# Two-layer graph network on one core: basis values and window numbers of the first edge loop kept in PSUM

## The reference

```
p     = clip(edge_attr_2, 0, 1)                       # 400000 x 2
b     = max(1 - |p[:, :, None] - (0, .5, 1)| * 2, 0)  # hat functions, 400000 x 2 x 3
basis = einsum('ea,eb->eab', b[:, 0], b[:, 1])        # reshaped to 400000 x 9
messages = einsum('ek,ei,kio->eo', basis, x[src], weight)
out   = zeros.at[dst].add(messages) / max(degree, 1) + x @ root_w.T + root_b
x     = layernorm(x + out)
```

## Time and profile before

| | us |
|---|---|
| median of 3 runs | 12081.59 |
| lowest and highest run | 12078.36, 12100.39 |
| profiled execution: span | 11991.0 |
| of it, first edge loop, first gather to the end of the last one | 4691.3 |
| of it, second edge loop (window 5060 to 11960) | 6900 |
| PE busy | 7745.6 (65%) |
| DVE busy | 7532.1 (63%) |
| POOL busy | 6643.3 (55%) |
| ACT busy | 817.6 (7%) |

### The profile page before, as it was taken

How to read it: one execution, slowest core, us unless ns; L and a number is a source line. 1 busy time by engine, 2 the same in 40 slices (tenths; PEclk the granted TensorE clock), 3 DMA queues, 4 the chain that set the end, 5 groups by cost and what they waited for, 6 DMA issues and landing times. The chain is left out here.

```text
span 11991.0 us, 122458 instructions
## 1 busy us (share of the span) xinstructions
PE 7745.6 (65%) x35701; PEld 5552.3 (46%) x35701; DVE 7532.1 (63%) x14033; ACT 817.6 (7%) x1907; POOL 6643.3 (55%) x6757
## 2 busy tenths in 40 slices
PE   5777777777777777455555555555555555555555
PEld 5777777777777777322222222222222222222223
DVE  4333333333333333588888888888888888888887
ACT  0000000000000000000000000000000000000000
POOL 5777777777777777044444444444444444444443
PEclk5555555555555555577777777777777777777776
DMA  1000000000000000011111111111111111111111
GB/s 36 11 11 11 11 11 11 11 11 11 11 11 11 11 11 11 37 39 36 39 36 39 36 39 36 39 36 39 37 39 37 39 37 38 37 38 37 38 37 29
DMA packets 251980, 327.74 MB, mean 27 GB/s; under 512 B 110894, under 2 KB 160959, under 8 KB 251087
## 3 DMA queue, kind: packets, MB, share of 16 engines
q0 software_dynamic: 200000, 205.20, 9.1%
q1 hardware_dynamic: 51962, 122.31, 3.2%
HBM read 320.67 MB, written 6.40 MB: 27 GB/s over the span
## 5 line engine op out<-in xcount | busy, mean ns | idle before, releaser
L411 PE MATMUL sums_ps<-hot,spread 128*96 128x64 f32 (+1 forms) x18750 | 3183.6, 370 | 1075.5 <-DVE spread L361 1075.5
L411 PEld LDWEIGHTS sums_ps<-hot,spread 128*96 128x96 f32 (+1 forms) x18750 | 3068.2, 281 | 1221.4 <-DVE spread L361 650.7
L361 DVE TENSOR_TENSOR spread<-basis,rows 128x1440 f32<-128x1440 f32 x625 | 1039.8, 1664 | 3215.1 <-DMA rows<-in_x,idx_a 1902.4
L754 PE MATMUL radial_x<-edge_t,hidden 128*128 128x384 f32 x3750 | 1916.7, 664 | 1211.3 <-DVE edge_t L856 1121.4
L282 POOL DMA_INDIRECT rows<-table_dram,idx_a x1875 | 1772.3, 945 | 1484.6 <-DVE prods_y L856 889.6
L282 POOL DMA_INDIRECT rows<-in_x,idx_a x1875 | 2140.3, 1141 | 634.2 <-issue 533.3
L754 PE MATMUL radial_y<-edge_t,hidden 128*128 128x384 f32 x2500 | 1377.7, 689 | 1509.5 <-DVE prods_y L856 1509.5
L754 PEld LDWEIGHTS radial_x<-edge_t,hidden 128*128 128x128 f32 x3750 | 886.1, 252 | 1856.0 <-issue 920.2
L282 POOL DMA_INDIRECT rows<-in_x,idx_b x1250 | 1422.4, 1138 | 443.7 <-issue 342.8
L282 POOL DMA_INDIRECT rows<-table_dram,idx_b x1250 | 1188.9, 951 | 766.7 <-DVE prods_y L856 363.0
L754 PEld LDWEIGHTS radial_y<-edge_t,hidden 128*128 128x128 f32 x2500 | 555.7, 246 | 2273.4 <-DVE prods_y L856 2014.4
(11 more groups left out here) (121 smaller groups left out, 3794.7 us busy)
## 6 DMA issues: line engine op xcount, KB each, us to landing
dist<-in_edge_weight SPq DMA_DIRECT2D x625, 160.0 KB, 3.2
rows<-in_x,idx_a POOLq DMA_INDIRECT x1875, 2.4
rows<-table_dram,idx_a POOLq DMA_INDIRECT x1875, 2.5
rows<-in_x,idx_b POOLq DMA_INDIRECT x1250, 2.4
rows<-table_dram,idx_b POOLq DMA_INDIRECT x1250, 2.5
acc<-in_edge_attr SPq DMA_DIRECT2D x1, 4687.5 KB
table_dram<-edge_t SPq DMA_DIRECT2D x1, 4687.5 KB
acc<-in_edge_attr SPq DMA_DIRECT2D x1, 3125.0 KB
```

Of the source, the lines that this page charges most:

```text
L361: dve.tensor_tensor(spread[s][:, :, 0:K].rearrange("e t (k c) -> e t k c", c=C), basis[s][:, :, :].unsqueeze(3).to_broadcast([P, G, 9, C]) ...
L411: last = pe.matmul(sums_ps[s][0:m, c * WINDOW:(c + 1) * WINDOW], spread[s][:, j, c * CH:c * CH + m], hot[s][:, j, :], start=(j == 0 and c ...
L754: last = pe.matmul(radial[h][:, j, 0:R], hidden[s][:, (j0 + j) * P:(j0 + j + 1) * P], w2p[:, :], start=True, stop=True)
```

## The change

A seventh PSUM bank, `own_ps`, is added for the first edge loop. Its first 64 columns hold the row of window numbers, copied there once per pass (there is one pass); the next 3 x 45 columns hold the three buffers of `basis`. So `basis` is written to PSUM, `hot` reads `window` from PSUM and `rel_t` from SBUF, and `spread` reads `basis` from PSUM and `rows` from SBUF. `basis` itself still reads two views of `edge_t` in SBUF. The order of the instructions in the loop, the waits and the buffer counts stay as they are; ahead of the loop there is one copy of 64 elements and a wait for it.

```diff
         rows = ring("rows", [P, G, C])
-        basis = ring("basis", [P, G, 9])
         spread = ring("spread", [P, G, K + 1])
...
-        gathers_begun = sem("l0_gathers_begun")
+
+        own_ps = ctx.enter_context(nc.psum_tensor("own_ps", [P, 512], F32))
+        window_ps = own_ps[:, 0:WINDOW]
+        basis = [own_ps[:, WINDOW + n * 9 * G:WINDOW + (n + 1) * 9 * G].rearrange("e (t k) -> e t k", k=9) for n in range(SLOTS)]
+        gathers_begun, window_ready = sem("l0_gathers_begun"), sem("l0_window_ready")
...
-                dve.tensor_tensor(basis[s][:, :, :].rearrange("e t (a b) -> e t a b", b=3),
+                dve.tensor_tensor(basis[s].rearrange("e t (a b) -> e t a b", b=3),
                                   f[:, :, 0:3].unsqueeze(3).to_broadcast([P, G, 3, 3]),
                                   f[:, :, 3:6].unsqueeze(2).to_broadcast([P, G, 3, 3]), ALU.mult).then_inc(basis_ready, 1)
-                dve.tensor_tensor(hot[s][:, :, :], keep["window"][:, :].unsqueeze(1).to_broadcast([P, G, WINDOW]),
+                dve.tensor_tensor(hot[s][:, :, :], window_ps.unsqueeze(1).to_broadcast([P, G, WINDOW]),
                                   rel_t[:, tiles].unsqueeze(2).to_broadcast([P, G, WINDOW]), ALU.is_equal).then_inc(hot_ready, 1)
                 dve.wait_ge(basis_ready, done(g, u))
                 dve.wait_ge(rows_landed[s], filled(g, u, 16 * G))
                 dve.tensor_tensor(spread[s][:, :, 0:K].rearrange("e t (k c) -> e t k c", c=C),
-                                  basis[s][:, :, :].unsqueeze(3).to_broadcast([P, G, 9, C]),
+                                  basis[s].unsqueeze(3).to_broadcast([P, G, 9, C]),
                                   rows[s][:, :, :].unsqueeze(2).to_broadcast([P, G, 9, C]), ALU.mult).then_inc(spread_ready, 1)
...
                 next_pass(dve, keep, step, p * 2 + steps)
+                dve.tensor_copy(window_ps, keep["window"][:, :]).then_inc(window_ready, 1)
+                dve.wait_ge(window_ready, p + 1)
```

## The result

The changed kernel is slower: 12667.19 us, the median of 4 runs (12659.8 to 12669.73), against 12090.99 us for the kernel before in its own 4 (12078.36 to 12107.45). The ratio is 1.0473, 95% interval 1.0457 to 1.0488. The forecast was 11470 us.

The account below looks back on a forecast made before the run. POOL's own instruction row was taken to bound the first loop; undelayed gathers give -612.7 us, rounded -612, all other terms 0, so 12081.6 - 612 = 11470 us, range 11440 to 11595.

Parts of the forecast that it names:

- `basis` doesn't fall on gathers: First loop: `basis`, still with two SBUF inputs, was taken to miss the gathers, 0 us; at most +119 if hit.
- a free step: First loop: with the delays gone, POOL needs 6.53 us a step, against 7.51 before the change.
- The rival by which the hold stays: First loop: something else in `spread` keeps the gathers long, nothing moves, 12082 us; chance 4%.
- 1.4 x 625: Slower rival: repeated PSUM reads make `spread` five times as long in the first loop, +890 us, 12970; chance 1%.
- Who is next: First loop: POOL at 6.53 us a step still bounds after the change, PE needing 5.80 us.
- stays clear: First loop: POOL never waits for a `rows` buffer; `spread` ends 3.2 us behind, POOL asks 6.25 us later.
- -610: First loop: cross-check by steps, 625 x 6.53 = 4081 us against 4691.
- the forecast's start: Whole kernel: median time before the change, 12081.6 us, from which 612 us were subtracted.
- PE takes over: First loop: PE's step grows from 5.80 to 6.9 us, losing 230 us (11700); 6% together with the `basis` case.
- The span lies 90.6 us below the median; I keep that difference.: Whole kernel: the 90.6 us between profiled span 11991.0 and median 12081.6 was kept unchanged in the forecast.

Follow-up runs that it names:

- e3: Kernel before with only `window` moved to PSUM, `basis` left in SBUF: 11989.33 us, against 11987.24 for the kernel before beside it.
- k1: Changed kernel, POOL free for 315 steps, then filling 1000 floats after each of 310 steps' gathers: 11656.46 us, against 11994.61 for the kernel before.
- e4: Changed kernel with PE summing only two of the five tiles of each step: 11390.39 us, first loop 4086.0 us.
- f4: Changed kernel with POOL filling 1500 floats (1.37 us) after each step's gathers, in the late condition: 12179.11 us.
- f1: The kernel before, unchanged, run again for its trace in the late condition: 12088.58 us, first loop 4782.9 us.
- e6: Changed kernel with POOL filling 600 floats (0.6 us) after each step's gathers: 12413.93 us, against 12086.91 for the kernel before.
- h1: Changed kernel with POOL filling 250 floats after every gather: 12050.79 us, against 11989.31 for the kernel before.
- e1: Kernel before, all in SBUF, with `spread` computing only 160 of 1440 elements: 11431.02 us, against 11987.24 for the kernel before.
- g3: Changed kernel with each first-loop gather replaced by a POOL fill of 1000 floats: 10945.0 us, first loop 3632.4 us.
- the first group: Four single runs, of the kernel before or the changed one with further edits, made together where the kernel before took 11987.24 us.
- g1: Changed kernel with PE summing two of five tiles, the same program as e4, in the late condition: 12618.38 us, first loop 5302.6 us.
- g4: Changed kernel with the 1.37 us pause of f4, plus 4000 plain DMAs issued by SP: 12193.25 us.
- f3: Same program as e1 (all in SBUF, `spread` cut to 160 of 1440 elements), in the late condition: 12412.46 us.

## Why the prediction was wrong

**Right:** that the first loop was bounded by POOL's row; that `spread` with two SBUF inputs held the gathers and with one in PSUM doesn't (mean 1141 to 946 ns, longest 2433 to 1267); that `hot` alone changes nothing (e3); that `spread` keeps its length (median 1659 before, 1647 after) and `basis` doesn't fall on gathers (three over 1.0 us in 3125, all before 125 us); that a free step costs 6.53 us (6.54 in k1) and the loop about 4081 (4086.0 in e4). The rival by which the hold stays fell. The Trainium skill, in "SBUF — State Buffer", section "Who interferes with whom", infers that a `tensor_tensor` doesn't hold up descriptor generation. The traces disagree: with two SBUF inputs `spread` held the gathers (mean 1141 ns), with one it doesn't (946), and nothing else of it changed. One slip in the rivals' sums, 1.4 x 625 given as 890 where it is 875, changes nothing.

**Wrong, first:** the part "Who is next", in two steps. I took PE's 5.80 us a step from the rows where it doesn't wait and gave it to a PE beside an unheld POOL, as if the two had nothing to do with each other; and I put POOL's wait for a `rows` buffer at nothing ("stays clear"), which supposes that PE's signals reach DVE at once. In the late condition they don't: `add` stood 2683.1 us for late signals of PE, POOL stood 1267 us for `spread`, and a step rose to 5358.3 / 625 = 8.57 us. POOL's holds, the very cost that I was taking away, had been what broke the runs of gathers (1.42 us in the step of rows 4); f4, where a pause of 1.37 us takes their place, has none of the long waits. The price that the sum lacked is 5358.3 - 4081 = +1277 us, and -610 + 1277 is the +667 that the loop shows. Added to the forecast it would give 11470 + 1277 = 12747 us; 12667 was measured, because the forecast's start, 12081.6, already held some 92 us of the same lateness. The rival "PE takes over" had the right victim, but a ceiling of 11700 and a cause that isn't the one found.

**Wrong, second:** "The span lies 90.6 us below the median; I keep that difference." Those 90.6 us were no overhead. In each run made for this study the time is 1.8 us above its span. The profiled execution was made in the quiet condition (its records are complete), the three runs, by their times, in the late one, and f1 shows where such a difference sits: in this very loop, as "remote" waits. A difference of 0.75% where the runs agree within 0.2% was a reason to ask, and to widen the range upward.

**Open:** what the late condition is. It goes with the session, since one chip had both. Nor do the runs say by what path POOL's gathers hold up PE's signals and instructions: their descriptors, their traffic, their completion signals, or something else of theirs. Every execution with a span here was also recorded, and in each late one records are missing, so the recording may well take part; then the loss of 4.7% would belong to recorded executions. There is no run without recording to decide it. The Trainium skill says in "NOTIFIC — the notification-queue block", section "7.1 Overflow: three behaviours, one of which stalls the engine", that the internal pipeline for such records holds its producers back rather than lose one, which could stall an engine. No run here shows whether it did. Nor was the threshold found: 0.6 us of pause in five gathers leaves the lateness (e6), 1.37 us leaves no long waits (f4), and 0.95 us ran only in the quiet condition. Whether it is the pause or the lower mean rate of gathers that helps isn't separated either; h1, which was to do it, also met the quiet condition.

## What to carry to other kernels

A delay that one engine suffers can be what keeps another one undisturbed: before taking it away, ask what rate it has been limiting, and run the kernel at that rate by a cheaper means (here e1 and g3, which cut work instead of moving it). Put the unchanged and the changed kernel themselves into every group of runs: the first group lacked the changed one, and so seemed to refute theory A. And where the profiled span and the timed median differ by more than the runs do among themselves, they may not be the same condition, and the difference is part of the question. Before reading waits from a trace, see whether its records are complete.

## What the hardware showed that I had not expected

- While POOL issues gathers every 1.25 us without a break, in some sessions PE's instructions come 0.7 or 1.4 us apart from about 12 us after the run's start until some 3 us after its last gather (timeline of after).
- In the same stretches a signal from PE to ACT can take 15.6 us with both engines idle (g1), and late signals begin earlier than slow instructions, some 7 us after the run's start (timeline of after).
- POOL's own unbroken work without gathers (g3) does nothing of this. Four times the DMA traffic, the added part issued by SP beside paused gathers (g4), causes no long waits but makes each recorded signal of PE's sums late, by 0.57 us in the median.
- In the late executions 40 to 81% of the records of the first loop's completion signals are missing, in the quiet ones at most 1%.
- The same program took 11431.02 us in one session and 12412.46 in another (e1 and f3), while the kernel before, in the same two, moved by less than 1% (11987.24 and 12077.02).
